# Experts' first weights fetched before the attention ends, the router's small tensors in PSUM, and expert results added into the output by the scatter

## What is computed

```
x = x + tanh(g_xattn[1]) * xattn(layernorm(x), ctx)     # ends with a LayerNorm, scale and bias
X = layernorm(x)
logits = X @ Wg + bg                                     # 8 experts
topv, topi = top_k(logits, 2)
w = softmax(topv)
out = X
for e in range(8):                                       # hidden size 1024
    h = silu((X*w) @ W1[e]) * ((X*w) @ W3[e])            # for each of a token's two places
    y = h @ W2[e]
    out = out + where(topi == e, y, 0).sum(places)
x = x + tanh(g_ffn[1]) * out
```

## Time and profile before

| what | value |
|---|---|
| median of 3 runs | 2014.66 us (2013.09 to 2015.47) |
| the profiled execution | 2012.49 us |
| its span in the profile | 2010.8 us |
| TensorE busy | 1795.7 us, 89% |
| VectorE busy | 1208.9 us, 60% |
| ScalarE busy | 1117.6 us, 56% |
| GpSimd busy | 432.7 us, 22% |
| first instruction of `experts` | about 1537.4 us |
| last matmul | about 1985.2 us |

### The profile page before, as it was taken

The page is one execution under the profiler, slowest core; times in us unless marked ns, Lnnn a source line. Parts: engine busy times, 40 slices in busy tenths (PEclk is TensorE's granted clock), DMA queues, the critical chain, the costliest instruction groups (busy, mean ns, idle before and its releaser), DMA issues. The chain is left out here.

```text
span 2010.8 us, 28118 instructions
## 1 busy us (share of the span) xinstructions
PE 1795.7 (89%) x9516; PEld 1121.8 (56%) x9516; DVE 1208.9 (60%) x2895; ACT 1117.6 (56%) x2332; POOL 432.7 (22%) x435
## 2 busy tenths in 40 slices
PE   5899998998997589999999999899986989999994
PEld 3555554554543234444544454345435889999994
DVE  3868777776784455445554455545653885555554
ACT  2466666666666146554454445454543657667662
POOL 3010210110101100000010002000203566776762
PEclk8899999999999699999998999899998999999997
DMA  3000000000000590000000000000004647666644
GB/s 94 1 22 1 11 11 1 1 22 1 1 1 1 205 308 1 22 0 1 1 22 1 0 1 23 22 1 1 21 2 143 218 134 249 204 200 212 217 151 141
DMA packets 122862, 134.13 MB, mean 67 GB/s; under 512 B 9248, under 2 KB 116640, under 8 KB 122720
## 3 DMA queue, kind: packets, MB, share of 16 engines
q1 hardware_dynamic: 115696, 119.45, 18.6%
q0 software_dynamic: 3744, 10.49, 1.4%
q10 hardware_dynamic: 3280, 2.40, 0.4%
HBM read 101.63 MB, written 30.69 MB: 66 GB/s over the span
## 5 line engine op out<-in xcount | busy, mean ns | idle before, releaser
L823 DVE TENSOR_REDUCE l_tile_max<-psum 128x1 f32<-128x512 f32 x512 | 342.0, 688 | 110.2 <-PE psum L546 108.6
L684 ACT ACTIVATE l_probs<-psum 128x1024 f32<-128x1024 f32 x256 | 248.3, 1022 | 96.8 <-PE psum L558 93.4
L546 PE MATMUL psum<-l_kT,l_qT 128*128 128x512 f32 x512 | 238.1, 472 | 40.1 <-DVE l_tile_max L823 36.7
L2257 POOL TENSOR_TENSOR moe_w_lo<-moe_w,moe_w_hi 128x512 fp32r<-128x512 f32 x184 | 240.7, 1309 | 148.3 <-ACT moe_w_hi L2044 147.5
L1548 DVE TENSOR_REDUCE l_row_max<-psum 128x2 f32<-128x1024 f32 x128 | 156.4, 1222 | 178.0 <-PE psum L1183 177.4
L1384 ACT ACTIVATE l_null_p<-l_s_null,l_neg_max 128x1 f32<-128x1 f32 x256 | 73.8, 288 | 295.5 <-DVE l_neg_max L1550 295.5
L1977 PE MATMUL psum<-moe_xs_hi,moe_w_hi 128*128 128x256 f32 x736 | 212.5, 289 | 5.7 <-POOL moe_w_lo L2257 5.7
L1977 PE MATMUL psum<-moe_xs_lo,moe_w_hi 128*128 128x256 f32 x736 | 210.2, 286 | 0.0
L1977 PE MATMUL psum<-moe_xs_hi,moe_w_lo 128*128 128x256 f32 x736 | 210.0, 285 | 0.0
L1386 ACT ACTIVATE l_probs<-psum,l_neg_max 128x512 f32<-128x512 f32 x256 | 171.8, 671 | 0.0
L546 PEld LDWEIGHTS psum<-l_kT,l_qT 128*128 128x128 f32 x512 | 98.2, 193 | 131.7 <-DVE l_tile_max L823 111.2
(11 more groups left out here) (278 smaller groups left out, 3278.9 us busy)
## 6 DMA issues: line engine op xcount, KB each, us to landing
moe_w<-in_moe_w SPq DMA_DIRECT2D x276, 256.0 KB, 4.9
moe_sorted_x<-l_zeros SPq DMA_DIRECT2D x1, 17680.0 KB, 57.1
moe_xs<-moe_sorted_x SPq DMA_DIRECT2D x23, 272.0 KB, 2.8
l_ctxT<-in_ctxT SPq DMA_DIRECT2D x4, 1024.0 KB, 5.6
x_resid<-in_x SPq DMA_DIRECT2D x4, 512.0 KB, 10.1
l_raw<-in_ctx SPq DMA_DIRECT2D x4, 512.0 KB, 3.3
l_v_raw<-in_ctx SPq DMA_DIRECT2D x4, 512.0 KB, 3.3
l_wk<-in_wkv SPq DMA_DIRECT2D x1, 2048.0 KB, 15.9
```

What stands on the lines that cost most here:

```text
L546: nc.tensor.matmul(bank(max_bank(m)), qT[:, q % SLOTS, h, t * P:(t + 1) * P], kT[:, q % SLOTS, h // 2, half * BANK:(half + 1) * BANK], sta ...
L684: nc.scalar.activation(probs[:, n % PT_RING], wide(2 * (n % 2)), ACT.Exp, scale=SCALE).then_inc(exp_done, 1)
L823: nc.vector.reduce_max(tile_max[:, q % 2, t, h, half:half + 1], bank(max_bank(m)), AX_X).then_inc(max_read, 1)
L2257: nc.gpsimd.tensor_tensor(w13_lo[:, k % SPLITS], w13[:, slot_k, :, cols], w13_hi[:, k % SPLITS].bitcast(F32), ALU.subtract).then_inc(w13_s ...
```

## The change

Four things are changed.

1. The two weight buffers, the row buffer and their semaphores move into a class `Stream` that lives through both blocks. In `layer1` the same memory holds the attention's weights (`wk`, `wv`, `wq`) and the context. When these are spent, SP loads the 8 pieces of tiles 0 and 1 and their rows there, as the last thing in its list of `layer1`; the loads before it in `experts` are gone.
2. In `experts`, the LayerNorms' and the router's small tensors lie in PSUM (banks 2 and 3), and the counts' matmuls write bank 7. In `layer1` they stay in SBUF. The prefix sum over experts is a masked product and a reduction. The last LayerNorm's `bn_stats` move to the end of `layer1`, its refinements behind the first splits, and its scaled copy `rows` is not made: `add_output` works in the banks.
3. The table `moe_y` is gone. The residual of batches 0 to 2 is stored to the output in `layer1`, that of batch 3 at tile 7 (`base_stored`). `store_results` scatters with an add into the output, the gate being applied in `evacuate_y`; rows that pad a tile get an index out of bounds and are dropped. Everything behind the last tile's scatters is gone.
4. In `layer1`, the tile tables of batches 0 to 2 are made in one go at `(7, 0)`, ahead of `keep_null_probs`.

```diff
@@ class Router: sum_tiles
-        nc.vector.tensor_copy(self.sums[:, 0, :], self.n_tiles[:])
-        src, d = 0, 1
-        while d < E:
-            dve.drain()
-            nc.vector.tensor_copy(self.sums[:, 1 - src, 0:d], self.sums[:, src, 0:d])
-            nc.vector.tensor_tensor(self.sums[:, 1 - src, d:E], self.sums[:, src, d:E], self.sums[:, src, 0:E - d], ALU.add)
-            src, d = 1 - src, 2 * d
+        nc.vector.tensor_tensor(self.below[:], self.n_tiles[:].unsqueeze(1).to_broadcast([P, E, E]), self.lower_expert[:],
+                                ALU.mult)
+        dve.drain()
+        nc.vector.reduce_sum(self.earlier_tiles[:], self.below[:], AX_X)
+        dve.drain()
+        nc.vector.tensor_tensor(self.last_tile[:], self.n_tiles[:], self.earlier_tiles[:], ALU.add)
@@ layer1, SP, behind its last context load
+                for b in range(ROUTED):
+                    sp.wait_ge(residual_added, b + 1)
+                    sp.dma_start(out[b].rearrange("(t p) n -> p t n", p=P), tokens(b)).then_inc(g["base_stored"], 16)
+                sp.wait_ge(listed, 1)
+                sp.wait_ge(misc_psum, last_fill("k", GROUPS - 1))
+                for m in range(stream.W_SLOTS):
+                    if m * stream.PIECE % s.FT == 0:
+                        e = stream.expert_of(sp, m * stream.PIECE // s.FT)
+                    stream.load_weights(sp, m, e)
+                    if m == 1:
+                        sp.wait_ge(scattered, 16 * TOP * T * ROUTED)
+                        stream.load_rows(sp, 0)
+                        stream.load_rows(sp, 1)
@@ layer1, VectorE, at (7, 0)
                             router.count_tiles(dve, ROUTED * T, ROWS - 1)
-                        if at == (7, 1):
                             router.sum_tiles(dve)
                             note_used()
-                        if at == (7, 2):
                             router.list_experts(dve, 0, s.FIRST)
-                        if at == (7, 3):
                             router.list_starts(dve, 0, s.FIRST)
-                            router.end_starts(0, s.FIRST)
+                            router.end_starts(0, s.FIRST).then_inc(listed, 1)
@@ experts, SP
-                sp.wait_ge(scattered, 16 * TOP * TB * LAST_B)
-                load_rows(0)
-                for m in range(PIECES):
+                for m in range(W_SLOTS, PIECES):
                     i, part = divmod(m * PIECE, FT)
                     if part == 0:
                         if i == FIRST:
                             sp.wait_ge(tiles_ready, 1)
+                        if i == FIRST + 2:
+                            sp.wait_ge(base_ready, 1)
+                            sp.dma_start(out[LAST_B].rearrange("(t p) n -> p t n", p=P), last_tokens).then_inc(base_stored, 16)
...
-                all_stored(sp)
-                for b in range(NB):
-                    load_results(sp, 0, b)
-                for b in range(NB):
-                    sp.wait_ge(fin, b + 1)
-                    sp.dma_start(out[b].rearrange("(t p) n -> p t n", p=P), block_rows(g["x"], b)).then_inc(stored, 16)
-                sp.wait_ge(stored, 16 * NB)
+                sp.wait_ge(base_stored, 16 * NB)
+                for i in range(TILES - 2, TILES):
+                    tile_stored(sp, i)
@@ experts, VectorE
                 def evacuate_y(i):
                     dve.wait_ge(y_psum, i + 1)
                     if i >= 2:
-                        dve.wait_ge(y_stored[i % 2], 16 * HALVES * (i // 2))
-                    nc.vector.tensor_copy(y_sb[:, i % 2].rearrange("p h d -> p (h d)"), y_bank(i)).then_inc(y_ready, 1)
+                        tile_stored(dve, i - 2)
+                    nc.vector.tensor_scalar(y_sb[:, i % 2].rearrange("p h d -> p (h d)"), y_bank(i), g["gates"][:, 3:4], None,
+                                            ALU.mult).then_inc(y_ready, 1)
...
+                small_end = [TB * E]
+                router.place_small(take_small)
...
-                dve.wait_ge(g["out_psum"], TB)
-                for _ in norm_out.statistics_steps(dve, lambda t: bank(t)[:, 0:D], LN_OUT_EPS):
-                    pass
+                rest = norm_out.after_stats(dve, LN_OUT_EPS)
+                next(rest)
                 split_down(0)
                 split_rows(0)
-                for t in range(TB):
-                    last = nc.vector.scalar_tensor_tensor(out=rows[:, t, :], in0=bank(t)[:, 0:D],
-                                                          scalar=norm_out.mv[:, t, 0:1], in1=g["ln_scale"][:],
-                                                          op0=ALU.subtract, op1=ALU.mult)
-                last.then_inc(out_read, 1)
+                next(rest)
@@ experts, GpSimd
                 def store_results(i, h):
                     if h == 0:
                         pool.wait_ge(y_ready, i + 1)
+                        if i in (0, FIRST):
+                            pool.wait_ge(base_stored, 16 * (LAST_B if i == 0 else NB))
+                        if i >= 1:
+                            tile_stored(pool, i - 1)
                     nc.gpsimd.indirect_dma_start(
-                        out=y_dram, out_offset=bass.IndirectOffsetOnAxis(ap=places[:, i % 3, h:h + 1], axis=0),
-                        in_=y_sb[:, i % 2, h, :], in_offset=None).then_inc(y_stored[i % 2], 16)
+                        out=out_rows, out_offset=bass.IndirectOffsetOnAxis(ap=places[:, i % 3, h:h + 1], axis=0),
+                        in_=y_sb[:, i % 2, h, :], in_offset=None, bounds_check=OUT_ROWS - 1, oob_is_err=False,
+                        compute_op=ALU.add).then_inc(y_stored[i % 2], 16)
```

304 lines of the change are left out of this document (181 added, 123 removed).

## The result

The changed kernel takes 1995.22 us (median of 4 runs, 1989.12 to 1997.73), the kernel before 2015.07 us (median of 4, 2013.09 to 2016.38). The ratio is 0.9895, with a 95% interval of 0.9871 to 0.9918: 20 us faster, where 31.5 were forecast. 1995.2 lies 1.2 us above the top of the range, 1994; as a ratio it lies on it (1994 over the 2014.66 known then is 0.9897). The profiled execution took 1997.42 us, its span is 1995.6.

What follows compares the result with a forecast made beforehand. TensorE was taken as the bound (89% busy), with gains possible only in the start, routing and end: 2 + 11 + 18.5 = 31.5 us. From 2012.49 that gave 1981.0, as a median 1983 us, range 1973 to 1994.

Steps and rivals of the forecast that it cites:

- 59% case: The main forecast for the whole kernel: 31.5 us gained, 1983 us, given a 59% chance.
- start: From the attention's last matmul to the first down matmul: preloaded weights give 7.0 us, holding the block up costs 5.4.
- routing and tile 5's rows: Small tensors in PSUM and a shorter prefix sum save 11 us of routing; the rows' fetch behind it stays the same.
- steady: Tiles 5 to 22, with TensorE busy without a gap: unchanged at 17.7 us per tile.
- end: Behind the last matmul: 20.9 us of loads, VectorE passes and stores go, less 2.4 for the add: 18.5 us.
- 0.8 of each: In the routing stage, 22.2 us of VectorE waiting against 18 lost, so each us of waiting removed gains 0.8.
- PSUM does not free VectorE, or the waits only change place among what stays: Rival on the routing: 31.5 us less 9 or more, 1992 to 1994 us; 12%.
- The adding scatters of tiles 0 to 21 are hidden: All tiles' scatters but the last: GpSimd waits for them only 13 us on, so they cost nothing.
- one more trip of 2.40 us: At the end, the last adding scatter lands 2.40 us later than a plain one, since it must read first.
- PSUM slow to reach: Rival on the routing: small instructions take longer in PSUM, 2.3 us less gain, 1985 us; 8%.
- The adding scatters pace the tiles: Rival on the tiles: GpSimd waits for landings, lengthening each tile from a landing of 12.4 us; 2048 us at 15; 4%.
- late but hidden: Rival on the adding scatters: they land after 5 to 13 us, only the end pays, 1985 to 1992 us; 7%.

Runs made afterwards that it cites:

- e2: The changed kernel with SP's loads of tiles 0 and 1 back at the start of the experts' block; 1991.9 us.
- e1: The changed kernel with the rows' loads of tiles 0 and 1 issued behind all eight pieces of weights; 1988.8 us.
- e4: The changed kernel with the scatters of results writing in place of adding; 1986.2 us.
- e3: The changed kernel with the norms' and the router's small tensors kept in SBUF; 2001.1 us.
- e7: e1 with VectorE's conversion of a tile's places in two instructions of one column in place of one of two columns; 1981.0 us.
- e5: e1 with a drain on GpSimd ahead of each of the splits of the first 40 steps; 2007.6 us.
- e11: The changed kernel run and profiled once more, nothing altered, beside a kernel with three further edits; 1992.6 us.
- e6: e1 with tile 2's two result scatters on GpSimd 4 steps later; 1986.6 us.

## Why the prediction was right and where it was wrong

Faster was right. The 59% case, 31.5 us, didn't come: the stages of the changed kernel's three profiles, without the attention, give 19.6 to 20.3 us, against 19.9 in the medians, which have the attention in them. By its own steps, each against the profile of before:

| step | forecast | measured |
|---|---|---|
| start | 2 (-3 to 7) | 0.1, 1.3, 1.4 |
| routing and tile 5's rows | 11 (6 to 14.8) and 0 (-2) | 5.9, 4.2, 4.2 |
| steady | 0 | -1.7 |
| end | 18.5 (10 to 20.9) | 16.0 |
| attention | 0 | -5.2, -5.2, 0.1 |

- **The start: right in its mechanism, a little too good.** SP holds the block up. The forecast had 5.7 us between the last matmul and the start and 13.6 from there to the first down matmul; measured are 7.7 and 13.1. Of the 2 us more, 0.8 are the landing and SP's start behind the last scatter (3.2 us from its issue in place of 2.4), 0.4 SP's issues (14.7 for 14.3), 0.5 that the last scatter is issued 10.5 us ahead of the attention's end and not 11.0, 0.3 the barrier. Inside the 13.1 us two errors cancel: step 0's product began 8.8 us behind the block's start and not 10.3, the splits waiting for nothing, and from there to the first down matmul it was 4.2 us and not 3.3. That the preload gives back what the hold costs is shown by e2, and that the hold is the place of the rows in SP's queue by e1.
- **The routing: the step that failed.** "So 22.2 us of such waiting go with 18 lost: 0.8 of each" took each wait away for good. The small forms that went to PSUM did what was forecast, 0.16 to 0.43 us each. But their waits came from GpSimd's splits, which have to be run all the same, and VectorE's own 35 splits met them instead: they wait 7.9 us more, where 14.8 were freed, some 5 of the 7.9 also with plain scatters (e4). The rival "PSUM does not free VectorE, or the waits only change place among what stays", 12% and 1992 to 1994 us, is the one that came nearest: it happened by half. e3 sizes what PSUM gives: 5.2 to 6.9 us, not 9.7 (11 less the prefix sum's 1.3). The profile of before has the granted clock's fall in the middle of the stage as well (0.95 over it), so its like among the changed kernel's are the two with 4.2 us; 1.7 of the first one's 5.9 are the clock's chance.
- **The adding scatters in the routing: not in the sum.** "The adding scatters of tiles 0 to 21 are hidden" looked at their landing and at GpSimd's share over the steady stage. Their issue takes 0.56 us longer, GpSimd has six of them and eight scatters of rows beside its splits in this stage, and where these fall together, from 1617.4 to 1648.1 in the changed kernel, it is busy 27.1 of 30.7 us and falls behind: 3 us by e4. The prediction's "I take 11" and "0 to -2" for tile 5's rows both suffer from it.
- **The steady stage: a missed term of 1.7 us.** A conversion of two columns (part of the change, though its list leaves it out), met by a split of GpSimd, and the longer scatters make a product late by 0.1 us per tile. Neither alone does (e4, e7): the scatter brings GpSimd's split later, the conversion is held to its end, and VectorE's split then meets the next one.
- **The end: right in what goes, wrong in what stays, and 2.5 us too good.** 9.6 us remain in place of 7.1. The second scatter begins 1.1 us later (0.56 for the first one's issue, the rest GpSimd's waits ahead of it), and from its start to the end of the span are 6.2 us, where 4.8 were taken. The 4.8 were a plain landing and "one more trip of 2.40 us" for the add. That trip isn't there: the last two adding scatters landed 2.7 us behind their issue, and e4's plain ones leave the same 4.7 us behind the last issue's end. What fills the time instead is 3.5 us behind the landing in which no engine works; the forecast had counted all of the 20.9 us as gone. What they are is not shown (in e5 they were 1.2 us fewer). That the two errors are of like size is luck.
- **PSUM slow to reach: no.** The page VectorE: DVE Perf Modes of the Trainium skill has 62 cycles more for an operand in PSUM. A 128x4 multiplication took 171 ns there (L148) where the like one in SBUF (L125, above) took 163; the measurement decides, and the cost is 0.01 us, not 0.065. What the page SBUF — State Buffer of the Trainium skill says under who interferes with whom, of one SBUF input outside the two-port modes, agrees with the forms that got an operand in PSUM, as with the earlier trace rows. Forms with their input and result in SBUF waited even with one input: the conversion of two columns 0.73 us (e7), the rows' scaling 816 ns (L2205).
- **The adding scatters pace the tiles: no.** Tiles take 17.8 us. From issue to landing it was 4.3 us (median of the steady stage's 38; the plain ones before 3.0), far from the 12.4 of this rival, and short of the 5 of "late but hidden".
- **The attention** is outside the change. It ended between 1530.1 and 1542.3 us in the fourteen profiles, among them 1542.3, 1542.3 and 1537.0 for one and the same kernel. The clock at its start isn't enough to tell them apart (e11), and ahead of it the first profile had the lower clock too: 0.97 and 0.76 in the windows 400 to 500 and 600 to 684 us, where e11 had 1.00 and 0.80. What sets the clock's moments stays open. Executions of one kernel lie up to 15 us apart (before: 2003.7 to 2018.5 over the four groups), more than the three runs shown ahead of the prediction had let expect; that the clock is the reason is likely, but only one execution of each run has a profile.

## What to carry to other kernels

When one engine's instructions wait for another engine's, the waits come from that engine's work and not from the instructions that happen to meet it. Moving these out of the way frees only so much as the instructions that stay don't wait in their place. A preload at the end of a block costs what it adds to that block's slowest queue, so what depends on a late event goes last in the queue, behind all that could go at once (3.5 to 7.4 us here). A longer issue on an engine with time to spare counts where its work bunches (27.1 of 30.7 us here), though its share of the whole stage (61.8 of 93.5) says nothing of it. And before a stage's microseconds are put down to an edit, look at its granted clock in both profiles: the same kernel took 93.4 us at 0.97 and 95.1 at 0.95.

## What the runs showed of the hardware

- An indirect scatter that adds keeps GpSimd 1.55 us, a plain one 0.99 (e4), for 128 rows of 1 KB. It landed 4.3 us behind its issue (changed kernel, steady stage), a plain one 3.0 (before).
- GpSimd's splits in a row leave VectorE's SBUF-only instruction no gap: 4.96 us behind three (changed kernel), 3.7 behind two (e6), up to 2.3 behind one with a scatter ahead of it (changed kernel, 1619.68).
- A drain on GpSimd costs nothing to be seen behind a split (the splits begin 1.44 to 1.64 us apart with it), and with a scatter ahead of it the next split begins 2.6 us or more behind the scatter's start (e5).
- A VectorE conversion of 128x2 from SBUF to SBUF took 0.73 us in the steady stage, held to the end of a GpSimd split, and 0.28 where that split ended sooner (e4). Two of 128x1 inside the same split took 0.14 each (e7).
